# Eight PSUM banks dealt out anew: two for pieces of projections and two for scores, where there were one and three

## The reference, cut to what matters

```python
# layer A, plain attention, then layer norm
q, k, v = x @ Wq.T + bq, x @ Wk.T + bk, x @ Wv.T + bv        # 16 heads of 16
attn = softmax(q @ k.T / 4) * head_mask
x = layernorm(x + (attn @ v) @ Wo.T + bo)
# layer B, causal attention with rotary embedding, then a mixture of 8 experts
n = rmsnorm(x) * g1
q, k = rope(n @ wq), rope(n @ wk);  v = n @ wv
h = x + softmax(where(causal, -inf, q @ k.T / 4)) @ v @ wo
m = rmsnorm(h) * g2                                             # top 2 of 8 experts by m @ w_router
x = layernorm(x + h + sum_of_two(w_e * (silu(m @ wg_e) * (m @ wu_e)) @ wd_e))
```

## Time and profile before

| what | value |
|---|---|
| median of 3 runs | 1528.28 us (1528.12 to 1532.54) |
| the profiled execution's own time | 1529.67 us |
| its span | 1527.9 us |
| TensorE matmuls busy | 1283.7 us, 84% of the span |
| VectorE, ScalarE, GpSimd busy | 968.6, 829.9, 698.7 us |

### The profile page before, as it was taken

How to read it: one execution, slowest core, us unless ns; L and a number is a source line. 1 busy time by engine, 2 the same in 40 slices (tenths; PEclk the granted TensorE clock), 3 DMA queues, 4 the chain that set the end, 5 groups by cost and what they waited for, 6 DMA issues and landing times. The chain is left out here.

```text
span 1527.9 us, 33404 instructions
## 1 busy us (share of the span) xinstructions
PE 1283.7 (84%) x11533; PEld 710.7 (47%) x11534; DVE 968.6 (63%) x1778; ACT 829.9 (54%) x1669; POOL 698.7 (46%) x717
## 2 busy tenths in 40 slices
PE   1799999999999999999999831499999999999910
PEld 0222232223223444444443311388888888888810
DVE  6478888888897888787877317443444434444446
ACT  3148888888878777666666620143443334443313
POOL 2324374546455756666564442524443344433312
PEclk9779999999999999999998865599999999999965
DMA  4417576766675878678666438292111111111136
GB/s 122 83 40 169 160 171 177 193 172 180 178 183 170 232 219 222 198 186 225 205 176 163 147 123 238 54 324 70 45 45 45 41 43 46 45 45 41 39 119 222
DMA packets 162442, 212.23 MB, mean 139 GB/s; under 512 B 28576, under 2 KB 124320, under 8 KB 162336
## 3 DMA queue, kind: packets, MB, share of 16 engines
q1 hardware_dynamic: 154848, 190.38, 45.2%
q0 software_dynamic: 7488, 20.46, 4.4%
HBM read 119.55 MB, written 82.58 MB: 132 GB/s over the span
## 5 line engine op out<-in xcount | busy, mean ns | idle before, releaser
L982 ACT ACTIVATE a_probs<-a_ps_s 128x512 f32<-128x512 f32 (+2 forms) x896 | 460.1, 569 | 172.6 <-PE a_ps_s L777 167.3
L1051 DVE TENSOR_REDUCE a_shift_max<-a_ps_m 128x1 f16<-128x512 f32 x512 | 320.7, 684 | 71.0 <-PE a_ps_m L782 69.7
L782 PE MATMUL a_ps_m<-a_qkx 48*128 48x128 f16 (+3 forms) x1408 | 287.0, 304 | 16.9 <-DVE a_shift_max L1051 8.4
L1568 PE MATMUL e_ps_gu<-e_xT,w_up 128*128 128x256 f16 x2574 | 298.1, 274 | 1.5 <-ACT e_xT L1623 1.4
L777 PE MATMUL a_ps_s<-a_qkx 49*128 49x128 f16 (+3 forms) x1408 | 277.9, 298 | 16.5 <-ACT a_probs L982 14.9
L1568 PEld LDWEIGHTS e_ps_gu<-e_xT,w_up 128*128 x2574 | 249.6, 98 | 35.0 <-issue 5.4
L878 PE MATMUL a_ps_o<-a_probs,a_v_one 128*32 128x512 f32 (+3 forms) x2048 | 237.2, 537 | 2.8 <-ACT a_o L989 2.7
L777 PEld LDWEIGHTS a_ps_s<-a_qkx 49*128 49x128 f16 x1408 | 90.7, 95 | 272.8 <-ACT a_probs L982 156.4
L1530 POOL DMA_INDIRECT y<-e_y,e_put x78 | 77.1, 988 | 250.0 <-DVE e_y L1657 238.1
L1668 DVE TENSOR_TENSOR e_h<-e_gate,e_ps_gu 128x512 f32<-128x512 f32 (+2 forms) x156 | 82.7, 551 | 136.8 <-ACT e_gate L1631 119.0
L1590 PE MATMUL e_ps_y<-w_down,e_h 128*128 x1404 | 162.7, 273 | 7.7 <-issue 5.2
(11 more groups left out here) (191 smaller groups left out, 1617.8 us busy)
## 6 DMA issues: line engine op xcount, KB each, us to landing
a_qkx<-a_qk_dram SPq DMA_DIRECT2D x192, 128.0 KB, 4.3
a_qk_dram<-a_qk SPq DMA_DIRECT2D x32, 512.0 KB, 5.5
a_o_dram<-a_o SPq DMA_DIRECT2D x64, 256.0 KB, 2.7
a_o_half<-a_o_dram SPq DMA_DIRECT2D x32, 256.0 KB
a_inv_half<-a_inv_dram SPq DMA_DIRECT2D x32, 256.0 KB
part<-a_part SPq DMA_DIRECT2D x16, 512.0 KB, 5.7
a_q_swap<-a_q SPq DMA_DIRECT2D x64, 128.0 KB, 3.9
c_rows<-y SPq DMA_DIRECT2D x16, 512.0 KB, 5.4
```

What stands on the lines that cost most here:

```text
L782: return pe.matmul(out, qx[first:first + 48, r, pair, q * P:(q + 1) * P], kx[first:first + 48, r, pair, k0:k1], start=start, stop=stop)
L982: act.activation(dst, src, ACT.Exp).then_inc(exp_out, 1)
L1051: vector.tensor_reduce(out, src, AX.X, ALU.max, negate=True).then_inc(max_out, 1)
L1568: mm = pe.matmul(ps_gu[:, bank, kind, f % 2], w[:, ds(e, 1)].rearrange("p o f -> p (o f)"), xT[:, s, xh, k, :], start=n == 0, stop=n == 5)
```

## The change

Pieces get two banks, `ps_x0` and `ps_x1`, and take turns by their number. Each bank has its own semaphore for "emptied", and a piece waits for the piece two before it. Scores lose a bank: score k goes to bank k % 2 and waits for the exponential of score k - 2. Maxima, `ps_o`, the order of every engine's list and every instruction's shape stay. The core of the diff (the rest of it puts `[numbers[...] % 2]` behind every use of `ps_x`, `ps_x16` and `piece_out`):

```diff
     def emptied_piece(engine, *piece):
-        engine.wait_ge(piece_out, numbers[piece] + 1)
+        engine.wait_ge(piece_out[numbers[piece] % 2], numbers[piece] // 2 + 1)
...
-        ps_s, ps_m = ps("ps_s", [P, 3, S], F32), ps("ps_m", [P, 3, S], F32)
-        ps_o, ps_x = ps("ps_o", [P, S], F32), ps("ps_x", [P, S], F32)
+        ps_s, ps_m = ps("ps_s", [P, 2, S], F32), ps("ps_m", [P, 3, S], F32)
+        ps_o, ps_x = ps("ps_o", [P, S], F32), [ps(f"ps_x{i}", [P, S], F32) for i in range(2)]
...
-                if numbers[piece] > 0:
-                    pe.wait_ge(piece_out, numbers[piece])
+                if numbers[piece] > 1:
+                    pe.wait_ge(piece_out[numbers[piece] % 2], numbers[piece] // 2)
...
-                if number >= 3:
-                    pe.wait_ge(exp_out, number - 2)
+                if number >= 2:
+                    pe.wait_ge(exp_out, number - 1)
...
-                bank = number % 3
+                bank = number % 2
...
-                    s_bank = number % 3
+                    s_bank = number % 2
...
-                src = ps_s[:, number % 3]
+                src = ps_s[:, number % 2]
```

More of the change, by code:

```diff
@@ L305, in attention_layers @@
         w_in, w_part = sb("w_in", [P, 2, WH], F32), sb("w_part", [P, 2, 2, WH], F16)
-        ps_s, ps_m = ps("ps_s", [P, 3, S], F32), ps("ps_m", [P, 3, S], F32)
-        ps_o, ps_x = ps("ps_o", [P, S], F32), ps("ps_x", [P, S], F32)
-        ps_x16 = ps_x[:].bitcast(F16)
-        x_loaded, xT_hi, xT_lo, piece_mm, piece_out = map(sem, (
-            "x_loaded", "xT_hi", "xT_lo", "piece_mm", "piece_out"))
+        ps_s, ps_m = ps("ps_s", [P, 2, S], F32), ps("ps_m", [P, 3, S], F32)
+        ps_o, ps_x = ps("ps_o", [P, S], F32), [ps(f"ps_x{i}", [P, S], F32) for i in range(2)]
+        ps_x16 = [x[:].bitcast(F16) for x in ps_x]
+        x_loaded, xT_hi, xT_lo, piece_mm = map(sem, (
+            "x_loaded", "xT_hi", "xT_lo", "piece_mm"))
+        piece_out = several("piece_out", 2)
         swapped, cos_out, sin_out, rope_out, qk_hi, qk_lo = map(sem, (
@@ L664, in project @@
                     for k in range(KD):
-                        mm = pe.matmul(ps_x[:], t.w_proj[:, 4 * layer + w, wh, k, m * P:(m + 1) * P],
+                        mm = pe.matmul(ps_x[numbers[("qk", u, c)] % 2][:], t.w_proj[:, 4 * layer + w, wh, k, m * P:(m + 1) * P],
                                        xT[:, u % 2, xh, k, :], start=n == 0, stop=n == 5)
@@ L675, in project_v @@
                         for k in range(KD):
-                            mm = pe.matmul(ps_x[:, j * D:(j + 1) * D], xT[:, u % 2, xh, k, q * P:(q + 1) * P],
+                            mm = pe.matmul(ps_x[numbers[("v", u, i)] % 2][:, j * D:(j + 1) * D], xT[:, u % 2, xh, k, q * P:(q + 1) * P],
                                            t.w_proj[:, 4 * layer + 2, wh, k, :], start=n == 0, stop=n == 5)
@@ L685, in turn_x @@
                         first = hl * D + k * P
-                        mm = pe.transpose(ps_x16[:, k * S + q * P:k * S + (q + 1) * P],
+                        mm = pe.transpose(ps_x16[numbers[("turn", u, hl)] % 2][:, k * S + q * P:k * S + (q + 1) * P],
                                           x_parts[:, q, first:first + P], t.ident16[:])
@@ L696, in turn_maxima @@
                 for q in range(QT):
-                    mm = pe.transpose(ps_x16[0:8, q * P:(q + 1) * P],
+                    mm = pe.transpose(ps_x16[numbers[("rows", u, c)] % 2][0:8, q * P:(q + 1) * P],
                                       shift_max[:, h % 2, q].rearrange("p o i -> p (o i)"), t.ident16[:])
@@ L708, in project_out @@
                         for k in range(KD):
-                            mm = pe.matmul(ps_x[:, j * D:(j + 1) * D], aT[:, u % 2, ah, k, q * P:(q + 1) * P],
+                            mm = pe.matmul(ps_x[numbers[("out", u, i)] % 2][:, j * D:(j + 1) * D], aT[:, u % 2, ah, k, q * P:(q + 1) * P],
                                            t.w_proj[:, 4 * layer + 3, wh, k, :], start=n == 0, stop=n == 5)
@@ L717, in turn_parts @@
                     for q in range(QT):
-                        mm = pe.transpose(ps_x16[:, k * S + q * P:k * S + (q + 1) * P],
+                        mm = pe.transpose(ps_x16[numbers[("parts", u, hl)] % 2][:, k * S + q * P:k * S + (q + 1) * P],
                                           part[:, q, hl, k * P:(k + 1) * P], t.ident16[:])
@@ L727, in route @@
                         for k in range(KD):
-                            mm = pe.matmul(ps_x[:, q * E:(q + 1) * E], nT[:, nh, k, q * P:(q + 1) * P],
+                            mm = pe.matmul(ps_x[numbers[("logits", u, 0)] % 2][:, q * E:(q + 1) * E], nT[:, nh, k, q * P:(q + 1) * P],
                                            t.w_router[:, wh, k, :], start=n == 0, stop=n == 5)
@@ L908, in move_qk @@
                 if causal(u):
-                    act.activation(q32[:, h % 2, w], ps_x[:], ACT.Copy).then_inc(piece_out, 1)
+                    act.activation(q32[:, h % 2, w], ps_x[numbers[("qk", u, c)] % 2][:], ACT.Copy).then_inc(piece_out[numbers[("qk", u, c)] % 2], 1)
                 else:
                     bias = (t.bk if w else t.bq)[:, c // 2:c // 2 + 1]
-                    act.activation(q32[:, h % 2, w], ps_x[:], ACT.Identity, bias=bias).then_inc(piece_out, 1)
+                    act.activation(q32[:, h % 2, w], ps_x[numbers[("qk", u, c)] % 2][:], ACT.Identity, bias=bias).then_inc(piece_out[numbers[("qk", u, c)] % 2], 1)
             def move_v(u, i):
@@ L920, in move_v @@
                 act.activation(v_one[:, u % 2, 2 * i:2 * i + 2, :, 0:DH],
-                               ps_x[:].rearrange("p (k h d) -> p k h d", k=2, d=DH), ACT.Copy).then_inc(piece_out, 1)
+                               ps_x[numbers[("v", u, i)] % 2][:].rearrange("p (k h d) -> p k h d", k=2, d=DH), ACT.Copy).then_inc(piece_out[numbers[("v", u, i)] % 2], 1)
             def move_rows(u, c):
@@ L927, in move_rows @@
                     act.wait_ge(rows_loaded[(h - 2) % 4], 32 * ((h - 2) // 4 + 1))
-                act.activation(rows[:, h % 2], ps_x16[0:8, 0:S], ACT.Copy).then_inc(piece_out, 1)
+                act.activation(rows[:, h % 2], ps_x16[numbers[("rows", u, c)] % 2][0:8, 0:S], ACT.Copy).then_inc(piece_out[numbers[("rows", u, c)] % 2], 1)
             def move_x(u):
@@ L932, in move_x @@
                 filled_piece(act, "v", u - 2, 1)
-                act.activation(xT[:, u % 2, 0].rearrange("p k s -> p (k s)"), ps_x16[:], ACT.Copy).then_inc(piece_out, 1)
+                act.activation(xT[:, u % 2, 0].rearrange("p k s -> p (k s)"), ps_x16[numbers[("turn", u, 0)] % 2][:], ACT.Copy).then_inc(piece_out[numbers[("turn", u, 0)] % 2], 1)
             def move_parts(u):
@@ L938, in move_parts @@
                     filled_piece(act, "logits", u - 1, 0)
-                act.activation(nT[:, 0].rearrange("p k s -> p (k s)"), ps_x16[:], ACT.Copy).then_inc(piece_out, 1)
+                act.activation(nT[:, 0].rearrange("p k s -> p (k s)"), ps_x16[numbers[("parts", u, 0)] % 2][:], ACT.Copy).then_inc(piece_out[numbers[("parts", u, 0)] % 2], 1)
             def empty_piece(n, i):
@@ L1111, in move_x @@
                     filled_piece(vector, "v", u - 2, 1)
-                    vector.tensor_copy(xT[:, u % 2, 1].rearrange("p k s -> p (k s)"), ps_x16[:]).then_inc(piece_out, 1)
+                    vector.tensor_copy(xT[:, u % 2, 1].rearrange("p k s -> p (k s)"), ps_x16[numbers[("turn", u, 1)] % 2][:]).then_inc(piece_out[numbers[("turn", u, 1)] % 2], 1)
             def move_parts(u):
@@ L1118, in move_parts @@
                         filled_piece(vector, "logits", u - 1, 0)
-                    vector.tensor_copy(nT[:, 1].rearrange("p k s -> p (k s)"), ps_x16[:]).then_inc(piece_out, 1)
+                    vector.tensor_copy(nT[:, 1].rearrange("p k s -> p (k s)"), ps_x16[numbers[("parts", u, 1)] % 2][:]).then_inc(piece_out[numbers[("parts", u, 1)] % 2], 1)
             def move_logits(u):
@@ L1125, in move_logits @@
                     vector.tensor_copy(t.logits[:, b * QT:(b + 1) * QT, :],
-                                       ps_x[:, 0:QT * E].rearrange("p (q e) -> p q e", e=E)).then_inc(piece_out, 1)
+                                       ps_x[numbers[("logits", u, 0)] % 2][:, 0:QT * E].rearrange("p (q e) -> p q e", e=E)).then_inc(piece_out[numbers[("logits", u, 0)] % 2], 1)
             def residual(u, i):
@@ L1132, in residual @@
                 x = x_res[:, u % 2, 2 * i:2 * i + 2]
-                y = ps_x[:].rearrange("p (q n) -> p q n", q=2)
+                y = ps_x[numbers[("out", u, i)] % 2][:].rearrange("p (q n) -> p q n", q=2)
                 if plain(u):
                     vector.wait_ge(biased, u + 1)
-                    vector.tensor_tensor(x, y, x, ALU.add).then_inc(piece_out, 1)
+                    vector.tensor_tensor(x, y, x, ALU.add).then_inc(piece_out[numbers[("out", u, i)] % 2], 1)
                 else:
@@ L1140, in residual @@
                         vector.wait_ge(part_lo, u)
```

(2 more changed lines are left out.)

## The result

| kernel | median | profiled execution's span | attention stage ends (first step of routing) |
|---|---|---|---|
| before | 1528.28 us | 1527.9 | 928.02 |
| changed | 1541.29 us (1534.99 to 1546.48) | 1537.8 | 936.15 |

The changed kernel is slower: ratio 1.0081, with a 95% interval of 1.0055 to 1.0107. The forecast was 1538.5. Ratios in this text compare mean times, and leave out two executions further on that took 1729 and 1726 us at a mean clock of 0.73.

A forecast was written before the change was run, and what follows sets the result against it. TensorE was taken to bound quarters with a long piece, score-bank waits for exponentials or late VectorE the others; 13.6 + 8.0 - 9.2 - 2.2 = +10.2 gave 1538.5 us, own range 1533 to 1545, 8 in 10 within 1527 to 1548.

The forecast's parts named there:

- The score bank in plain units: Plain units: five quarters without a long piece wait one exponential more, +1.87; with smaller terms +2.13 a unit.
- The piece bank in plain units: Plain units: second "out" piece no longer waits for `residual`, -0.33; three qk pieces no longer wait for ScalarE's emptying, -0.2.
- The score bank in causal units: Causal units: scores wait for exponentials, mainly in g3 (+0.68); about +1.1 a unit, +8 in all, bounds 0 and +22.
- The piece bank in causal units: Units 10 to 13, g2q3: second "out" piece no longer waits for `residual`; with two shorter waits elsewhere -9.2, bounds 0 and -13.8.
- The ends: Attention stage's start and end: second projection and last "out" half stop waiting; -0.8 at the start, together -2.2, bounds 0 and -4.
- gains don't come: Rival, causal units: "out" pieces start early but maxima behind them wait as long as now; +20, 1548 us, chance 0.17.
- the piece bank wins: Rival: GpSimd less late, full 13.8 back in causal units, score losses at low bounds; -12, 1516 us, chance 0.10.
- The falling clock: Rival: longer idle time in plain quarters without a long piece brings the clock to 1.2 GHz; 1578 us, chance 0.03.
- its three cases: Outcomes counted as slower: the forecast itself 0.58, gains don't come 0.17, the clock falling 0.03.

The follow-up runs named there:

- the score half: Against the kernel before: two banks for scores instead of three, one for pieces as before, the eighth bank unused; 1550.30 us, ratio 1.0153.

## Why the prediction was right, and where it was not

The measured time is near the forecast, and the largest mechanism, the score bank in plain units, is as predicted. But the terms for the causal units and for the ends were wrong, and that their errors cancel in part is luck.

- *The score bank in plain units* was the right mechanism, and its quarters came out to 0.01: 2.88, 2.88, 2.88, +0.49 in g2q0, 3.49 unmoved with a long piece. Eight units gave +14.2 for the half, against 2.13 x 8 = 17: a plain unit whose clock doesn't fall has +1.85. g1q2, reckoned at +0.13, gave nothing, g3q1 -0.1. Unit 6 even became 0.7 shorter: in the kernel before, its g2q1 took 4.45 with a clock of 0.50. In the three other traces with the same plain part it took 2.72 to 4.17, in the four with two score banks 2.88 each time.
- *The piece bank in plain units*: -0.33 once and -0.07 twice (g1q3 and g3q3), where -0.07 three times was worked out; -3.9 in all for -4.2.
- *The score bank in causal units*: g3 was +0.70 for +0.68, g0 +0.56 less 0.23 in unit 12 for +0.2. But the sum was +3.7 for +8. It has -8.6 in it from g2q3 of units 10 to 13, where TensorE came later and GpSimd was no longer late; the rest, +12.3, is more than was forecast.
- *The piece bank in causal units* is the step that failed: -9.2 was forecast, -0.3 measured. In the changed kernel g2q3 did fall, by 3.67, 2.15, 3.67 and 2.71 in units 10 to 13, 12.2 together, more than the 1.7 and 2.3 a unit that were worked out; the low clock behind such a wait costs 1.5 (6.92 for unit 10, 5.41 for unit 11, where it didn't fall), not 0.6. I read the wait as the bank's, since it ended when `residual` emptied it. It hung on GpSimd's order: moving `part_low` alone took away all four waits, and two of the four went away with the score half alone. What the bank had over the score half in g2q3, 3.6, was lost again in other quarters of the same trace: units 9, 11 and 12 each have 6.8 us at a clock of 0.50, in g1q1 and g2q1, which the score half doesn't have there (it has them in units 13 and 14 instead). I had looked for the clock only as a gain in g2q3.
- *The ends*: -5.5 in the trace for -2.2, -3.7 at the start for -0.8 and -1.8 at the end for -1.4. I had reckoned with the waits alone. At the start the projections close up, but the maxima behind them then wait for a DMA, and the score half's first maxima start only 0.1 later than the changed kernel's. What moved is the clock: a projection of 2.74 takes 1.47 where it is at 1.00. How much of this the second bank brings isn't shown: the clock first rose at 37 to 40 us in the six traces with a second piece bank at the start, and at 36, 36, 48, 69 and 93 us in the five with one.
- The errors cancel in part: causal sum +3.4 for -1.2, plain +10.3 for +13.6, ends -5.5 for -2.2, together +8.1 at the end of the stage for +10.2. The rest of the program took 1.7 more in this one execution; over the eleven traces it takes 599.5 to 602.9, and took 599.9 in the kernel before.
- Rivals: that gains don't come was right for the sum of the causal units, but not by its mechanism, since the maxima behind the "out" piece did not wait as long as before; it was wrong for the ends. The rival in which the piece bank wins had one premise right, that GpSimd would be less late in the new order. The falling clock did not decide here (mean clock 0.926, before 0.923), but it does with one score bank, where small idle times, 0.68 before each score, go with a clock of 0.59 to 0.72. The Trainium skill, "TensorE: Matmul & The Clock Gate", section "A second HAM failure mode: psum-queue depth-cycling", tells of such small idle times between groups of matmuls that cycle through PSUM banks, with the clock swinging between its two levels, and the trace of one bank agrees. With two banks and idle times of 0.47 to 0.97 the clock is 1.00 from 100 to 500 us in both traces of the changed kernel.
- One sum in the prediction is off: slower at 0.79 is more than its three cases make, 0.58 + 0.17 + 0.03 = 0.78.

Left open: why the clock falls behind the pause in g2q1 in some units and executions and not in others, and what the second piece bank does to the clock at the start; no run was made to part these causes.

## What to carry to other kernels

A bank in a rotation is worth what it evens out: reckon one quarter of the list with start, latency and release times from the timeline, once for each bank count, and ask which quarters have other work that covers the wait. Before giving a bank to a wait, ask who makes the last engine late: the same wait went away, for more, by moving one GpSimd instruction. And compare stretches of two traces only after you have seen how far two executions of one kernel differ there: at the start of the stage two traces with the same waits were 1.9 us apart by the clock alone. Last, a buffer can be lent where its owner is idle; the ends of the stage took the third score bank at no cost.

## What was not expected of the hardware

- In unit 12 of the changed kernel a pause of TensorE of 0.93 us for a score bank went with a clock of 0.50 for 6.8 us, during which the "out" half took 2.74 instead of 1.48. The cost of a wait was larger in what followed than in itself. It is not a rule of that pause: g2q1 of units 10 to 13 has it in all four, and in unit 13 of the same trace no fall follows.
- With pauses of 0.68 before each score the clock swung between its levels and the mean over the execution was 0.77; the plain units took 16 to 35% more than the 77.6 that the waits alone make, 8 to 25% more than the 84 with ScalarE's moves.
